# Moving the 65 tokens' tile to the front of its batch, with half of the next tile's keys beside it

## What is computed

```python
x = x + xattn(layernorm(x), ctx)   # 16 heads of 128, softmax over the 1601 tokens
x = x + causal_attn(layernorm(x))  # 16 heads of 32
x = x + ffn(x)                     # ternary weights, silu(gate) * up, rms norm
# xattn, per head:
q = rmsnorm(hidden @ Wq, gq);  k = rmsnorm(ctx @ Wk, gk);  v = ctx @ Wv
out = softmax(q @ k.T / sqrt(128)) @ v;  out @ Wo
```

## Time and profile before

| | us |
|---|---|
| median of 3 runs | 1468.04 (1466.3 to 1470.63) |
| the profiled execution | 1467.54 |
| its span on the core | 1465.7 |
| PE busy | 1437.7 (98%) |
| DVE busy | 1242.0 (85%) |
| ScalarE busy | 997.7 (68%) |
| GpSimd busy | 163.8 (11%) |

### The profile page before, as it was taken

One profiled execution on the slowest core, in us unless ns is written; L12 is line 12 of the kernel. 1 busy time (PEld: TensorE's weight loads), 2 busy tenths in 40 slices (PEclk: granted clock), 3 DMA queues, 4 the chain that ended last, 5 costly groups with the idle time before them and its releaser, 6 DMA issues.

```text
span 1465.7 us, 22223 instructions
## 1 busy us (share of the span) xinstructions
PE 1437.7 (98%) x6829; PEld 1180.9 (81%) x6829; DVE 1242.0 (85%) x1994; ACT 997.7 (68%) x3689; POOL 163.8 (11%) x119
## 2 busy tenths in 40 slices
PE   8999999999999999999999999999999988999998
PEld 7778878888888888788888887888888867887887
DVE  8746888999999999999999998988898999677543
ACT  5676777776877777677777775777667656547432
POOL 2200000002000200110020002000200210023342
PEclk9999999999999999999999999999999999999999
DMA  6542332322222133222322331221221142841000
GB/s 203 174 137 80 112 102 69 95 73 71 82 87 83 59 87 91 80 69 87 90 69 69 99 89 40 83 58 48 58 65 37 45 149 67 276 173 59 1 0 29
DMA packets 106405, 126.20 MB, mean 86 GB/s; under 512 B 10928, under 2 KB 80816, under 8 KB 105136
## 3 DMA queue, kind: packets, MB, share of 16 engines
q1 hardware_dynamic: 98992, 117.45, 26.0%
q10 hardware_dynamic: 7296, 7.34, 1.5%
HBM read 102.11 MB, written 22.64 MB: 85 GB/s over the span
## 4 chain that ended last, share of the span: by engine, by line
PE 76%; DVE 16%; issue 4%; ACT 2%; DMA 1%; SPq 0%; POOL 0%; DVEq 0%; POOLq 0%; ACTq 0%
PE ps L36 23%; PE ps L38 23%; PE ps L37 23%; DVE p_lo L42 3%; DVE ring L1241 3%; PE ps L983 2%; PE ps L984 2%; DVE ring L1209 2%; PE ps L1001 1%; PE ps L1002 1%; DVE k_sum L1166 1%; DVE w_q L1347 1%; ACT ps L1832 1%; DVE row_sum L1329 1%; PE ps L856 1%
## 5 line engine op out<-in xcount | busy, mean ns | idle before, releaser
L1832 ACT ACTIVATE ps<-ps 128x128 f32<-128x128 f32 x1212 | 316.7, 261 | 140.0 <-PE ps L38 138.6
L36 PE MATMUL ps<-wk_hi,cT_hi 128*128 128x512 f32 x808 | 315.4, 390 | 3.1 <-ACT ps L1832 1.6
L38 PE MATMUL ps<-wk_hi,cT_lo 128*128 128x512 f32 x808 | 314.4, 389 | 0.0
L37 PE MATMUL ps<-wk_lo,cT_hi 128*128 128x512 f32 x808 | 314.4, 389 | 0.0
L1832 ACT ACTIVATION_READ_ACCUMULATOR ps<-ps 128x1 f32 x1212 | 224.5, 185 | 0.0
L36 PEld LDWEIGHTS ps<-wk_hi,cT_hi 128*128 128x128 f32 x808 | 151.8, 188 | 38.2 <-issue 3.5
L38 PEld LDWEIGHTS ps<-wk_hi,cT_lo 128*128 128x128 f32 x808 | 151.7, 188 | 31.5
L37 PEld LDWEIGHTS ps<-wk_lo,cT_hi 128*128 128x128 f32 x808 | 151.7, 188 | 31.1
L36 PE MATMUL ps<-fq_hi,cT_hi 128*128 128x512 f32 x416 | 162.6, 391 | 2.1 <-DVE ring L1209 2.1
L37 PE MATMUL ps<-fq_lo,cT_hi 128*128 128x512 f32 x416 | 162.6, 391 | 0.0
L38 PE MATMUL ps<-fq_hi,cT_lo 128*128 128x512 f32 x416 | 162.4, 390 | 0.0
(11 more groups left out here) (244 smaller groups left out, 2660.3 us busy)
## 6 DMA issues: line engine op xcount, KB each, us to landing
cT_raw<-in_ctxT SPq DMA_DIRECT2D x96, 128.0 KB, 2.7
cn_raw<-in_ctx SPq DMA_DIRECT2D x96, 128.0 KB, 2.3
row_raw<-in_wgu SPq DMA_DIRECT2D x32, 256.0 KB, 2.8
w_raw<-in_wguT SPq DMA_DIRECT2D x32, 256.0 KB, 2.7
qk_scratch<-folded ACTq DMA_DIRECT2D x8, 896.0 KB, 4.5
fq_raw<-qk_scratch SPq DMA_DIRECT2D x14, 512.0 KB, 3.9
pc_scratch<-pc_out SPq DMA_DIRECT2D x7, 1024.0 KB, 4.2
w_scale<-scale_scratch SPq DMA_DIRECT2D x96, 64.0 KB, 2.7
```

Source lines behind the costliest of these rows:

```text
L36: pe.matmul(dst, l_hi, r_hi, start=first, stop=False)
L37: pe.matmul(dst, l_hi, r_lo, start=False, stop=False)
L38: return pe.matmul(dst, l_lo, r_hi, start=False, stop=last)
L1832: done = act.activation(head, head, ACT.Square, accum_out=k_sum[:, i, g * GH + h:g * GH + h + 1])
```

## The change

`rest_first` is true for b = 3, 5 and 7. In these batches the rest tile becomes t = 0 and the full tiles follow as t = 1 to 12; the sources of the two loads are shifted by one for that. The keyless steps are now 39, 65 and 91 (before: 51, 77 and 103). The tile before each of them (38, 64, 90) is still the one whose keys serve both rest tiles. In a keyless step PE has the two halves of the scores first, then key banks 0 and 1 of the next tile, then the context; the next step has only key banks 2 and 3. The last step has keys now, so the refinement of tile N - 1 is done before its scaling. The weight pieces of b = 2, 4 and 6 are at 3, 5, 6, 8, 9, 10, 11 and those of the other batches at 3, 5, 6, 8, 9, 11, 12. Nothing else is moved; the number of products, of DMA transfers and of pieces stays.

```diff
--- before.py
+++ after.py
@@ -138,20 +138,22 @@
         RING = 14
 
 
-        REST = TT - 1
-        assert TK == REST * P + P // 2 + 1 and B % 2 == 0 and 4 <= B <= P
+        assert TK == (TT - 1) * P + P // 2 + 1 and B % 2 == 0 and 4 <= B <= P
         tiles = [(b, t, P) for b in range(B) for t in range(TT)]
         N = len(tiles)
         halves = (slice(0, P // 2), slice(P // 2, P))
 
-
-        key_tiles = [s for s, (b, t, n) in enumerate(tiles) if t < REST or b < 2 or b % 2 == 0]
+        rest_first = [b % 2 == 1 and b >= 2 for b in range(B)]
+        rest_tile = [b * TT + (0 if rest_first[b] else TT - 1) for b in range(B)]
+
+
+        key_tiles = [s for s, (b, t, n) in enumerate(tiles) if s not in rest_tile or b < 2 or b % 2 == 0]
         key_of = {s: i for i, s in enumerate(key_tiles)}
         NK = len(key_tiles)
 
         cT_seq, cT_keys, cT_scores, cT_step = [], {}, {}, []
         for s, (b, t, n) in enumerate(tiles):
-            if t == REST and b >= 2 and s in key_of:
+            if s in rest_tile and b >= 2 and s in key_of:
                 cT_keys[s] = len(cT_seq)
                 cT_seq.append((s, True))
                 cT_step.append(s - 2)
@@ -343,7 +345,7 @@
         ROW_LEAD = 6
         piece_slots = list(range(ROW_LEAD + 1, TT + 1)) + [
             b * TT + t for b in range(1, B - 1)
-            for t in ((3, 5, 6, 8, 9, 11, 12) if b * TT + REST in key_of else (3, 5, 6, 8, 9, 10, 11))][:NP - TT + ROW_LEAD]
+            for t in ((3, 5, 6, 8, 9, 10, 11) if b >= 2 and rest_tile[b] in key_of else (3, 5, 6, 8, 9, 11, 12))][:NP - TT + ROW_LEAD]
         piece_at = {s: i for i, s in enumerate(piece_slots)}
         assert len(piece_at) == NP and max(piece_at) < N
 
@@ -441,7 +443,7 @@
 
         def refinements(s):
 
-            return sum(4 if tiles[k][1] == REST and tiles[k][0] >= 2 else 3 for k in key_tiles if k <= s)
+            return sum(4 if k in rest_tile[2:] else 3 for k in key_tiles if k <= s)
 
         def evacuations(b, part=None):
 
@@ -711,8 +713,12 @@
                 context = [(u - 1, c2) for u in steps[s] if u > 0 for c2 in range(KC)]
                 behind = BEHIND_BANK[len(context)] if s < N - 1 else ((0,), (1,), (), ())
                 for g in range(NG):
-                    if s in key_of and (s > 0 or g > 1):
+                    if s in key_of and (s > 0 or g > 1) and (s == 0 or s - 1 in key_of or g > 1):
                         key_bank(s, g)
+                    if s not in key_of and g == 2:
+
+                        key_bank(s + 1, 0)
+                        key_bank(s + 1, 1)
                     if s == 0 and g == 2:
                         for c in range(KC):
                             fold(NG - 1, c)
@@ -1182,7 +1188,7 @@
                 dve.scalar_tensor_tensor(out=w[:], in0=w[:], scalar=-0.5, in1=k_mean[:, i],
                                          op0=ALU.mult, op1=ALU.mult).then_inc(k_refined, 1)
                 dve.wait_ge(k_refined, done + 2)
-                if t < REST:
+                if s not in rest_tile:
                     dve.scalar_tensor_tensor(out=y, in0=w[:], scalar=1.5, in1=y,
                                              op0=ALU.add, op1=ALU.mult).then_inc(k_refined, 1)
                 elif b < 2:
@@ -1190,7 +1196,7 @@
                                              op0=ALU.add, op1=ALU.mult).then_inc(k_refined, 1)
                 else:
 
-                    dve.wait_ge(scaled, (b - 1) * TT + REST + 1)
+                    dve.wait_ge(scaled, rest_tile[b - 1] + 1)
                     for parity, rows in enumerate(halves):
                         dve.scalar_tensor_tensor(out=left_rstd[rows, parity], in0=w[rows], scalar=1.5, in1=y[rows],
                                                  op0=ALU.add, op1=ALU.mult).then_inc(k_refined, 1)
@@ -1434,6 +1440,7 @@
                     low_cn(EARLY_CN[s])
 
 
+            key_refine(N - 1)
             scale_scores(N - 1)
             track_max(N - 1)
             second = LAST + PART
@@ -1841,7 +1848,7 @@
                 act.wait_ge(k_guessed, 2 * k + 1)
                 if k >= 2:
                     before = key_tiles[k - 2]
-                    if tiles[before][1] < REST:
+                    if before not in rest_tile:
                         act.wait_ge(scaled, before + 1)
                     else:
                         act.wait_ge(k_refined, refinements(before))
@@ -2357,7 +2364,11 @@
                 b, t, n = tiles[tile]
                 if e >= 3:
                     sp.wait_ge(cT_lo_done, e - 2)
-                src = cT_v[b, :, :, t * P:(t + 1) * P] if t < REST else restT_v[B + b // 2 - 1 if keys_alone else b]
+                if tile in rest_tile:
+                    src = restT_v[B + b // 2 - 1 if keys_alone else b]
+                else:
+                    i = t - rest_first[b]
+                    src = cT_v[b, :, :, i * P:(i + 1) * P]
                 sp.dma_start(cT_raw[:, e % 3], src).then_inc(cT_in[e % 3], 16)
 
             def load_cn(i):
@@ -2365,8 +2376,12 @@
                 b, t, n = tiles[cn_seq[i]]
                 if i >= 3:
                     sp.wait_ge(cn_lo_done, i - 2)
-                sp.dma_start(cn_raw[:, i % 3, :], ctx[b, t * P:(t + 1) * P, :] if t < REST else rest[b]).then_inc(
-                    cn_in[i % 3], 16)
+                if cn_seq[i] in rest_tile:
+                    src = rest[b]
+                else:
+                    k = t - rest_first[b]
+                    src = ctx[b, k * P:(k + 1) * P, :]
+                sp.dma_start(cn_raw[:, i % 3, :], src).then_inc(cn_in[i % 3], 16)
 
             def load_fq(b, k):
                 sp.wait_ge(fq_lo_done, KC * b + k)
```

## The result

| | before | after |
|---|---|---|
| median | 1467.3 (1466.3 to 1470.63, 6 runs) | 1472.84 (1470.21 to 1473.95, 6 runs) |
| ratio after / before | | 1.0029, 95% interval 1.0018 to 1.0039 |
| the profiled execution | 1467.54 | 1472.70 |
| its span | 1465.7 | 1470.7 |

The change makes the kernel 0.29% slower; the forecast was 1472.2 us. The quotient of the two medians in the table is a little larger, 1.0038, and lies inside the interval. No change, a ratio of 1, lies outside the interval, but the ratio is just under the 0.3% that was taken as what a measurement tells. The busy times of the page, to be set beside the earlier trace rows: PE and DVE did the same instructions and took a little longer.

The account below looks back on a forecast made before the run. The kernel was taken as bound by PE, with DVE close behind. The terms -6.5 - 5.4 + 11.3 + 0.9 + 3.9 = +4.2 us took the profiled 1467.54 to 1471.7, and 0.5 more for the median gave 1472.2 us; range 1463 to 1477.

Parts of the forecast that it names:

- pauses of steps 51 and 77 go: In the old keyless steps: two PE waits for p_lo of 2.4 us and 1.7 us of slow clock vanish, -6.5 us.
- keys of one step moved to the last step: From step 91 to 103: 24 products of 0.227 us leave the part where PE sets the time, -5.4 us.
- pause at three changes of batch: Before the first key bank of steps 41, 67 and 93: PE pauses 4.1 us each, net 3.8, together +11.3 us.
- slow clock behind them: After the three new pauses: a slow stretch costing 1.3 us a place, +3.9 us.
- tail: Last step: VectorE's added key work for tile 103, less a removed wait of 0.56 us, +0.9 us; bounds -0.5 and +3.
- Part 1: Keyless step from t=12 to t=0 in batches 3, 5 and 7: -6.5 and -5.4 us, tail +0.9.
- Part 2: Two early key banks in the keyless step: six and six groups don't cover the change of batch, +11.3 us.
- Part 3: What the early keys need in the keyless steps: all ready before PE comes, p_lo stall gone, no cost.
- Part 4: Weight pieces moved off steps 38 and 64: 1.7 us of pause saved at two places, already counted; otherwise nothing.
- the one where the clock holds: Rival: same pauses at the changes of batch but no slow stretch, +0.3 us, 1468.3 us; chance 0.22 including no effect.
- the shorter pause: Rival: VectorE ahead at the change of batch, pause 1.8 us, no slow clock, -6.5 us, 1461.5 us; chance 0.18.
- the late one: Rival: col_sum pushed back, pauses 5.3 us, full slow stretch of 1.7 each, tail +2.5; +10.7, 1478 us; chance 0.13.

Follow-up runs that it names:

- e9: The changed kernel with the rest tile of batch 7 back at t=12, batches 3 and 5 as in the change; 1471.83 us.
- e5: The changed kernel with GpSimd's sum reduction on 64 columns instead of 1024, logarithm and refinement reading the unreduced sum (output not the block's); 1453.16 us.
- e3: The changed kernel with ScalarE's key squares ahead of exponential, logarithm and guess in steps with t=1; 1469.15 us.
- e1: The changed kernel without the two early key banks of the next tile in the keyless step; 1472.16 us.
- e2: The changed kernel with the weight pieces of batches 2 and 4 left at t=11 and 12 instead of 10 and 11; 1477.49 us.
- e6: The kernel before with only the early key banks 0 and 1 added in its keyless steps, rest tiles staying at t=12; 1462.90 us.
- e4: The changed kernel with GpSimd's sum reduction over partitions replaced by a copy (output not the block's); 1481.76 us.
- e10: e8 with the rest tile of batch 7 at t=5; 1458.33 us.
- e11: e10 with ScalarE's square of key bank 2 ahead of exponential, logarithm and guess in steps with t=1; 1457.71 us.
- e7: e6 with the weight pieces of batches 3 and 5 off t=11 too and two more pieces in batch 6; 1461.43 us.
- e8: The changed kernel with the rest tile at t=11 in batches 3 and 5, t=12 in batch 7, weight pieces as in e7; 1460.71 us.

## Why the prediction was right

By its terms, in the one profiled execution of each kernel:

| term | forecast | measured | from |
|---|---|---|---|
| pauses of steps 51 and 77 go | -6.5 | -6.5 | none in 598 to 632 and 880 to 914 |
| keys of one step moved to the last step | -5.4 | -5.5, as a remainder | 1192.70 against 1188.95, see below |
| pause at three changes of batch | +11.3 | +11.0: 3 x (3.93 + 0.1 - 0.37) | idle 3.78 plus what a product overlaps, 0.16 |
| slow clock behind them | +3.9 | +3.9 (1.3, 1.2, 1.4) | granted clock |
| tail | +0.9 | +0.8 | 5.56 against 4.73 |
| sum | +4.2 | +3.7 | |

The profiled executions differ by 5.2 us, more than the sum, and some of that lies outside the changed steps. The product after a pause at the end of the first batch, ahead of all that the change moves, and the one late in the tail, first of the kernel before, then of the changed one, both in TensorE's timeline:

```profile
208.03 0.50 PE L36 MATMUL ps<-wk_hi,cT_hi 128*128 128x512 f32 x1 [0.93 <-ACT ps L1832]
...
1206.11 0.50 PE L36 MATMUL ps<-p_hi,cx_hi 128*128 128x512 f32 x1 [1.59 <-DVE p_lo L42]
```

```profile
208.87 0.50 PE L36 MATMUL ps<-wk_hi,cT_hi 128*128 128x512 f32 x1 [1.02 <-ACT ps L1839]
...
1210.63 0.50 PE L36 MATMUL ps<-p_hi,cx_hi 128*128 128x512 f32 x1 [1.72 <-DVE p_lo L42]
```

Between these two the changed kernel takes 4.52 - 0.84 = 3.7 us more, which is the sum. At the maximum ahead of the last scaling it is 1192.70 - 1188.95 - 0.84 = 2.9 us behind; the other terms up to there are -6.5 + 11.0 + 3.9 = 8.4, so -5.5 are left for the 24 products. The other 1.5 us lie in stages that the change doesn't touch; what they are in the medians stays open.

That the forecast of 1472.2 is off by only 0.6 us is luck in part. The difference of the medians is 5.5 us where 4.2 was forecast; the forecast was counted from a median of three runs, 1468.04, which went down to 1467.3 with three more.

Part 1 holds: the two stretches of the changed kernel show that nothing is lost in steps 51 and 77, and e9 that batch 7 by itself is about even. Part 2 holds in its mechanism and its size: e5 shows that the sum's reduction is the cause, e3 that ScalarE's queue is the first gate and VectorE's chain the second. What part 2 leaves out is that second gate. The time doesn't show it, since TensorE, held at the first one, comes to key bank 2 of step 41 at 499.60, after that gate has opened (496.80 in e3). Part 3 holds, and e1 adds that what it priced was worth nothing. Part 4 holds: its 1.7 us are 1.7 by e2, where 0.6 of them went into a wait for p_lo and 1.05 into the pause. One reading of part 1 is off without changing the sum: over 889 to 893 not half of the stretch was at the lower level. A granted clock of 0.57, between levels of 0.5 and 1, is most of it.

Of the rivals, the one where the clock holds is out (it fell three times of three in the profiled execution), the shorter pause too (3.9 us, not 1.8), and the late one: the subtraction did not get ahead of col_sum, so the upper end of 5.3 us was not reached. The stall for p_lo is gone, so the change does what it says. The clock was no sure thing for shorter pauses: after those of 3.8 us in the change, e2 and e9 it fell six times of six, after 3.2 us in e1 and 2.6 in e3 twice of three times each.

The subtraction took 5.56 us under the full reduction and 1.26 under the short one of 0.79 us. The Trainium skill (SBUF — State Buffer, "SBUF: two separate sides") has the port pair go to whoever starts first, for the whole instruction, and of VectorE's instructions it names those with two SBUF inputs or in a two-port mode. The subtraction agrees with that, and the reduction of k_sum, which the prediction set against it, has one input and is no counterexample. Under col_max the trace differs, and there it decides: cn_lo, with two inputs, took 2.12 us instead of 0.42 but ended at 482.18, a microsecond before col_max's end at 483.23, and p_lo, also with two inputs and begun at 482.10, kept its 1.21 us.

My weakest step was in an expectation, not in the prediction: e6 assumed that the release after col_sum stays where it was, though which of two instructions is held decides whether 1.2 us follow it.

## What to carry to other kernels

Where one engine has less work in one step of a stream, put that step where the next engine is ahead, and not beside a reduction that holds it: the same saved work was free at t=11 and t=12 and cost 5 us at t=0. Count the groups between the last thing that starts the held chain and the first that needs its result; their order within hardly counts. A change made of several parts is worth running part by part: here one part alone (e6) gained 0.4%, and the move of the tile took that back and more.

## What the runs showed of the hardware that I had not expected

On GpSimd a plain instruction behind a partition reduction started 6.8 to 7.9 us late in this kernel (e4: seven times, 6.76 us of idle at step 39, with nothing that the profile shows it waiting for, ahead of a copy of 1.03 us), while a second reduction follows the first at once (483.13 behind 479.90 + 3.33). What it does in that time no run shows.

A reduction over partitions of 64 columns took 0.79 us at step 39 (0.79 to 1.61 over the kernel) beside 6.19 us for 1024, and under the short one VectorE's subtraction kept its speed.

The runs of the kernel before, with three pauses near 2 us, scatter more than those of e10: 1465.52 to 1471.14 in 17 runs, 1457.41 to 1458.86 in 5. That the slow clock follows such a pause in some executions only would explain it: in the profile before it followed one of the two equal pauses of the earlier trace rows. The clock on record fits: beside e1 to e4, the three shortest of the 16 runs of the kernel before (1465.99 to 1466.29) had a mean granted clock of 0.998 or 0.999, the three longest (1470.36 to 1470.84) 0.994 or 0.995. Beside e9 to e11 the order is less clean. But e6, e7 and e8, which keep one pause of 2.1 us in the tail, scatter no more than e10 (1.4 to 1.6 us in 4 or 5 runs). No run tested the explanation.
